# Eighty-four bursts of idle products between the expert layers of a four-layer sandwich kernel, in a new order of its pieces

## The reference, cut to what matters

```python
x = x + ln(L0_attn(ln(x)))   # Mamba scan, then a mixture of 8 experts, top 2
x = x + ln(L0_ffn(ln(x)))    # 64 small experts, top 8, and 2 shared ones
x = x + ln(L1_attn(ln(x)))   # WKV recurrence
x = x + ln(L1_ffn(ln(x)))    # ternary weight
x = x + ln(L2_attn(ln(x)))   # attention in a window of 32
x = x + ln(L2_ffn(ln(x)))    # one of 8 matrices by position
x = x + ln(L3_attn(ln(x)))   # Lorentz attention
x = x + ln(L3_ffn(ln(x)))    # 8 experts, top 2, and a shared one
```

```python
g, u = x2d @ gate_w[e].T, x2d @ up_w[e].T
out += wmat[:, e] * ((silu(g) * u) @ down_w[e].T)
```

## Time and profile before

| | |
|---|---|
| median of 3 runs | 1402.85 us (1395.88 to 1403.54) |
| the profiled execution | 1396.86 us |
| its span, first to last instruction | 1395.0 us |
| TensorE busy | 1118.2 us (80%) |
| VectorE busy | 964.1 us (69%) |
| ScalarE busy | 718.8 us (52%) |
| GpSimd busy | 599.6 us (43%) |
| mean granted TensorE clock | 0.915 |

### The profile page before, as it was taken

The page is one execution under the profiler, slowest core; times in us unless marked ns, Lnnn a source line. Parts: engine busy times, 40 slices in busy tenths (PEclk is TensorE's granted clock), DMA queues, the critical chain, the costliest instruction groups (busy, mean ns, idle before and its releaser), DMA issues.

```text
span 1395.0 us, 13322 instructions
## 1 busy us (share of the span) xinstructions
PE 1118.2 (80%) x3922; PEld 583.8 (42%) x3922; DVE 964.1 (69%) x2181; ACT 718.8 (52%) x1377; POOL 599.6 (43%) x420
## 2 busy tenths in 40 slices
PE   4766968796978797787877776878987899999796
PEld 1222323332333243333334534445463556656565
DVE  4965887678866885576777795747636535559787
ACT  6626663756347642534334425435561468746564
POOL 1941966178715873032014763543423121225222
PEclk8897979897998899698989999989998999999898
DMA  6000000000000001100010000000000100000000
GB/s 216 1 0 0 1 0 1 1 0 1 0 1 0 1 1 68 36 0 1 1 68 1 1 0 0 1 1 1 1 1 17 52 0 1 8 1 8 0 9 8
DMA packets 11271, 17.76 MB, mean 13 GB/s; under 512 B 1304, under 2 KB 7584, under 8 KB 10688
## 3 DMA queue, kind: packets, MB, share of 16 engines
q1 hardware_dynamic: 11200, 16.93, 3.7%
HBM read 15.88 MB, written 1.05 MB: 12 GB/s over the span
## 4 chain that ended last, share of the span: by engine, by line
PE 38%; DVE 11%; ACT 7%; issue 3%; POOL 3%; POOLq 0%; DVEq 0%; ACTq 0%
PE bankE L1878 6%; PE bankE L1263 4%; ACT b_pr L1161 2%; PE bankS L1841 2%; PE bankE L1795 2%; PE bankS L1795 2%; PE bankE L1325 2%; PE bankS L1826 2%; PE bankE L1284 1%; PE bankS L1798 1%; PE bankE L1798 1%; PE bankE L660 1%; PE bankS L1768 1%; PE bankE L615 1%; PE bankE L653 1%
## 5 line engine op out<-in xcount | busy, mean ns | idle before, releaser
L775 DVE TENSOR_TENSOR_SCAN hs<-dA,carry,bankS 128x512 f32<-128x512 f32 x118 | 144.4, 1265 | 3.0 <-DVE bankS L766 0.4
L351 POOL TENSOR_TENSOR hc<-hs,cb 128x1024 f32<-128x1024 f32 x51 | 120.2, 2356 | 33.3 <-DVE hs L775 31.8
L1753 ACT ACTIVATE c_h<-bankE,C 128x512 f32<-128x512 f32 x144 | 98.7, 687 | 52.7 <-PE bankE L1878 50.4
L1647 POOL TENSOR_TENSOR c_acc<-c_acc,c_tw 128x512 f32<-128x512 f32 x32 | 45.9, 1436 | 159.5 <-DVE c_tw L1972 159.4
L326 POOL TENSOR_TENSOR cv<-cv,hc 128x1024 f32<-128x1024 f32 x45 | 106.2, 2361 | 3.5
L467 ACT ACTIVATE sg<-bankE,C 128x512 f32<-128x512 f32 x80 | 54.9, 687 | 83.5 <-PE bankE L615 83.4
L1878 PE MATMUL bankE<-c_fH,c_w1H 128*128 128x512 f32 x144 | 81.1, 563 | 1.1 <-ACT c_h L1753 1.1
L660 PE MATMUL bankE<-hh,f 128*128 128x512 f32 x128 | 70.4, 631 | 10.0 <-DVE hh L882 10.0
L766 DVE TENSOR_TENSOR bankS<-dx,bankS 128x1024 f32<-128x1024 f32 x59 | 72.2, 1223 | 6.2 <-PE bankS L539 5.7
L420 ACT ACTIVATE dA<-dl,Aneg 128x512 f32<-128x512 f32 x118 | 74.3, 708 | 0.1
L578 PE MATMUL bankE<-h2T,wg 128*128 128x512 f32 x128 | 71.1, 638 | 3.6 <-ACT sg L448 1.4
(11 more groups left out here) (534 smaller groups left out, 2955.4 us busy)
## 6 DMA issues: line engine op xcount, KB each, us to landing
c_w<-in_w SPq DMA_DIRECT2D x1, 2304.0 KB, 8.9
X<-in_x SPq DMA_DIRECT2D x4, 256.0 KB, 4.0
wg<-in_gate_T SPq DMA_DIRECT2D x1, 1024.0 KB, 7.8
wu<-in_up_T SPq DMA_DIRECT2D x1, 1024.0 KB, 9.8
f<-in_w SPq DMA_DIRECT2D x1, 1024.0 KB, 7.5
out<-X SPq DMA_DIRECT2D x4, 256.0 KB, 2.3
b_wq<-in_Wqkv SPq DMA_DIRECT2D x1, 768.0 KB, 4.4
g<-in_sw SPq DMA_DIRECT2D x2, 256.0 KB, 3.5
```

The source lines that it names most:

```text
L351: pool.tensor_tensor(dst[:, :, :], hs[:, k % HS, :, :], cb[:, k % 2, :].unsqueeze(1).to_broadcast([P, HV, G]), ALU.mult).then_inc(s["hc_re ...
L775: V.tensor_tensor_scan(hs[:, k % HS, h, :], decay(i, k, q), drive[:, h, :], carry[:, k, h:h + 1], ALU.mult, ALU.add).then_inc(s["scan_done ...
L1753: act.activation(h[:, n % 3, :], E[k % 2][:, :], ACT.Gelu_apprx_tanh, bias=col("b1_3", k)).then_inc(s["fs_ready"], 1)
```

## The change

A new kind of piece, Z, belongs to TensorE alone: three products of a constant by a constant, written to `S[3]`, that nothing reads and that signal nothing. There are 24 of them (Z0 to Z23) for each of the groups 0, 1 and 2 and 12 (Z0 to Z11) for group 3, 84 in all. Z0 to Z11 stand behind L1 of their group, Z12 to Z23 behind L2. All other pieces are the same as before, in an order that was searched anew with the bursts in it, in all three lanes.

```diff
 ORDER = [(p[0], p[1:].split(".")[0], int(p.split(".")[1])) for p in """
...
-    aM9.0 ao4.1 aN5.1 aM10.0 an5.1 aM11.0 ao5.1 aN6.1 aM12.0 an6.1 aM13.0 ao6.1 aN7.1 an7.1 aM14.0 ao7.1 aM15.0 aA4.1 aA5.1 aA6.1 aL1.0
-    aL3.0 aA7.1 aN8.1 aL4.0 an8.1 ao8.1 aL5.0 aN9.1 an9.1 aR2.0 ao9.1 aU0.0 aN10.1 an10.1 aU1.0 aU2.0 ao10.1 aU3.0 aR5.0 aN11.1 an11.1
...
+    aM10.0 ao4.1 aN5.1 an5.1 aM11.0 aM12.0 aA3.1 ao5.1 aN6.1 aM13.0 aM14.0 an6.1 ao6.1 aM15.0 aL1.0 aA4.1 aA5.1 aL3.0 aN7.1 an7.1 aL4.0
+    aZ0.0 aZ1.0 ao7.1 aZ2.0 aZ3.0 aA6.1 aN8.1 aZ4.0 aZ5.0 aZ6.0 aZ7.0 an8.1 ao8.1 aL5.0 aN9.1 an9.1 aA7.1 aZ8.0 aZ9.0 ao9.1 aR2.0 aU0.0
...
@@ -255,6 +259,7 @@
     FOLD = 1
+    BURST = 3
     SPREAD = {2: (1, 0), **{2 * x_ - 1: (x_,) for x_ in range(2, E0N)}}
@@ -624,6 +629,9 @@
             elif p == "L2":
                 down1(e, N_U - 1)
                 pe.matmul(E[2][:, :], fb2[:, :], cwT[:, :], start=False, stop=True).then_inc(s["fo_ready"], 1)
+            elif p[0] == "Z":
+                for _ in range(BURST):
+                    pe.matmul(S[3][:, :], sel[:, 0, :], sel[:, 0:4, :].rearrange("p a b -> p (a b)"), start=True, stop=True)
             elif p == "L6":
```

More of the change, by code:

```diff
@@ L105 @@
[L105 to L120, removed]
@@ new lines @@
+    aU6.0 ao13.1 aN14.1 an14.1 aU7.0 ao14.1 aN15.1 aU8.0 aU9.0 an15.1 ao15.1 aU10.0 aU11.0 aU12.0 aB1.1 aU13.0 aB3.1 aB4.1 aU14.0 aB2.1
+    aF1.2 aU15.0 aU16.0 aF5.2 aU17.0 aU18.0 aF6.2 aU19.0 aF2.2 aF0.2 aL2.0 aF7.2 aF3.2 aF8.2 aR1.1 aZ12.0 aL6.0 aZ13.0 aZ14.0 aZ15.0 aZ16.0
+    aR3.1 aA0.2 aA1.2 aL7.0 aA2.2 aA3.2 aZ17.0 aZ18.0 aF9.2 aN0.2 an0.2 aM0.1 aZ19.0 ao0.2 aZ20.0 aZ21.0 aZ22.0 aR4.1 aZ23.0 aM1.1 aN1.2
+    an1.2 aM2.1 aM3.1 ao1.2 aN2.2 an2.2 aM4.1 aM5.1 ao2.2 aN3.2 an3.2 aM6.1 aM7.1 ao3.2 aN4.2 an4.2 aM8.1 aM9.1 ao4.2 aN5.2 an5.2 aM10.1
@@ new lines @@
+    aZ9.2 an8.3 ao8.3 aL5.2 aN9.3 an9.3 ao9.3 aR2.2 aU0.2 aU1.2 aU2.2 aR5.2 aN10.3 aZ10.2 an10.3 ao10.3 aN11.3 an11.3 aR6.2 aZ11.2 aU3.2
+    ao11.3 aN12.3 aU4.2 an12.3 aU5.2 ao12.3 aN13.3 aU6.2 an13.3 aU7.2 ao13.3 aU8.2 aN14.3 aU9.2 aU10.2 an14.3 aU11.2 ao14.3 aN15.3 aU12.2
+    an15.3 aU13.2 aU14.2 aU15.2 aU16.2 ao15.3 aB1.3 aU17.2 aB3.3 aB4.3 aU18.2 aU19.2 aB2.3 aL2.2 bP0.0 aR1.3 aL6.2 aZ12.2 aZ13.2 aZ14.2
+    aZ15.2 aZ16.2 bP1.0 aZ17.2 aZ18.2 aZ19.2 aL7.2 bP2.0 aR3.3 bP3.0 aR4.3 bP4.0 aM0.3 bP5.0 bK1.0 bK11.0 aZ20.2 aZ21.2 aZ22.2 bK2.0 bK3.0
@@ new lines @@
+    bH3.2 bA10.3 bW3.2 cG1.0 bO3.2 bQ0.3 bA1.2 bA11.2 bA12.2 cH0.0 cZ0.0 cZ1.0 bA3.2 bQ1.3 cE0.0 cZ2.0 cE1.0 cT0.0 bX0.2 bQ2.3 ct0.0 cZ3.0
+    cE2.0 cE3.0 cT1.0 bX1.2 bX2.2 bX3.2 bQ3.3 ct1.0 cT2.0 bX4.2 ct2.0 bX5.2 bX6.2 bX7.2 cT3.0 bA4.2 bA2.2 bC0.3 cS6.0 bc0.3 ct3.0 cZ4.0
+    cY0.0 bA13.2 bN0.3 bC1.3 bV0.3 cS7.0 bH0.3 bc1.3 bN1.3 cy0.0 cW0.0 bW0.3 cZ5.0 cE4.0 bO0.3 bC2.3 bV1.3 bH1.3 bc2.3 bW1.3 bO1.3 bN2.3
+    bC3.3 bV2.3 bH2.3 bc3.3 cV0.0 bW2.3 bN3.3 cZ6.0 cT4.0 bO2.3 bV3.3 bH3.3 bW3.3 ct4.0 bO3.3 bA1.3 bA11.3 cZ7.0 cE5.0 bA12.3 cX0.0 cT5.0
@@ new lines @@
+    cR3.2 cU2.2 cU3.2 cO1.1 cU4.2 cs8.0 cU5.2 cU6.2 cO2.1 cU7.2 cU8.2 cU9.2 cU10.2 cU11.2 cU12.2 cU13.2 cU14.2 cU15.2 cU16.2 cR0.3 cU17.2
+    cU18.2 cU19.2 cU20.2 cR1.3 cU21.2 cU22.2 cU23.2 cU24.2 cU25.2 cU26.2 cU27.2 cR2.3 cU28.2 cU29.2 cU30.2 cU31.2 cU32.2 cU33.2 cU34.2
+    cU35.2 cU0.3 cU1.3 cO0.2 cR3.3 cU2.3 cU3.3 cO1.2 cU4.3 cU5.3 cU6.3 cO2.2 cU7.3 cU8.3 cU9.3 cU10.3 cU11.3 cU12.3 cU13.3 cU14.3 cU15.3
+    cU16.3 cU17.3 cU18.3 cU19.3 cU20.3 cU21.3 cU22.3 cU23.3 cU24.3 cU25.3 cU26.3 cU27.3 cU28.3 cU29.3 cU30.3 cU31.3 cU32.3 cU33.3 cU34.3
@@ L149, in mamba_and_experts @@
+    cU35.3 cO0.3 cO1.3 cO2.3
+""".split()]
 def mamba_and_experts(s, X, C, col, S, E, ident, sel, half, dram, first_lane, second_lane, bank):
```

66 lines of the change are left out of this document (34 added, 32 removed).

## The result

The changed kernel takes 1420.62 us (median of 4 runs, 1418.04 to 1422.69), the kernel before 1403.19 us on the same chip. The ratio is 1.0137, with a 95% interval from 1.0108 to 1.0165: 19 us slower, outside the range and with the other sign.

What follows compares the result with a forecast made beforehand. Waits between TensorE and VectorE, with TensorE partly at half clock, were taken as the bound. Clock -20, bursts +5.5 and order -3.3 sum to -17.8 us, from 1402.85 to 1385 us; range 1362 to 1408 us.

Steps and rivals of the forecast that it cites:

- What bounds the kernel: Whole kernel: waits between TensorE (80% busy) and VectorE (69%), with TensorE at half clock for part of the span.
- The clock: Seven turns from one expert layer to the next: less TensorE work at half clock saves 20 us.
- the bursts: Same seven turns: bursts mostly fill TensorE's idle time; 0.5 us exposed in each of four, 1.2 in three, +5.5 us.
- Rival 2: Seven turns: the clock stays up but little of it is on the path; 1400 us, no change, chance 0.16.
- Rival 1: Seven turns: the clock falls despite the bursts, which run at half; 8.1 us lost per turn, 1417 us, chance 0.13.
- The order: Second turns: router work moved earlier saves 3.3 us; rest of the new order taken as 0, 10 us either side.
- Rival 3: Causal and last layers: the new order loses 15 to 25 us, giving 1400 to 1408 us, chance 0.08.
- What would show it: Seven turns mostly at full clock: mean about 0.95, router product about 1 us, first U 1.02, TensorE busy near 1143.
- three signs against: Bursts spaced 0.43 us; L5 or M1's gate product over 1 us later; longer time from the b pieces on.

## Why the prediction was wrong, point by point

**What bounds the kernel** held: waits between TensorE and VectorE, and a low clock behind the long ones.

**The clock** (-20 us) and **the bursts** (+5.5 us) sum to -14.5 us. In the new order they measured together -7.5 to -9 us, at 78 us less of half clock; so half of the expected sum came. In the old order the same bursts in the nearest places measured +25 us, and 62 others, put into the waits, -4 us; so the +5.5 us were a price of these places in this order and of no other. The estimate spread the gain over all seven turns. The sections show it in three and lie within 0.3 us in four: L1 to L2 of group 0 takes as long with the bursts as without, since the first `hh` comes at nearly the same time. Rival 2 was right for three of the four sections behind L1; the fourth, of group 3, won 2.6 us. Rival 1 was right in two turns, where the bursts ran at half: in group 1 L5 came 1.3 us and the first U 2.6 us later than without them, in group 3 the first U 3.6 us later. Neither section grew by more than 0.3 us by it. How much of the net is the clock's and how much the bursts' no run separates, since no kernel has the one without the other.

**The order**, the step that failed: "For all the rest of the order the trace gives no price; I take 0, with 10 us to either side". The whole term was -3.3 us; it measured +26 us, beyond its bound. The 3.3 us did not come either. The wait for the router's weights did fall in the changed kernel (from 11.5 us in four to 5.3 us in three), but mostly since bursts stand in it: with the order alone it was 3.48 and 3.21 us in the two like turns, before 3.95 and 4.42 us, and the weights came 1.1 and 5.2 us later after L2. And these are waits of a few us on one engine, while the pieces that moved with them are whole scan steps (3.7 us of VectorE, 4.7 us of GpSimd) and a Mamba front. The trace of before did give prices for those. The earlier trace rows show VectorE 92% busy in the first turn, so a step moved into it must delay what stands behind it by about its own 3.7 to 4.7 us (with that step alone moved, L5 and `c` each came 4.5 us later after L1), and I wrote that "VectorE does the same work", which is true of the engine and false for the path. The bound of 10 us was taken from waits to be saved, not from work that was moved. One step, the U row of one group and one Mamba front, each moved alone, cost 0.83%, 0.50% and 0.35%; that these moves make up the 26 us is not shown, since undoing one in the new order won nothing.

**Rival 3** (the order loses elsewhere, 15 to 25 us) had nearly the size and the wrong place: behind the last L2 the time did not grow (677.6 to 676.6 us). Its chance of 0.08 was the mistake that cost the range; it should have stood for lane a too, where pieces moved past an engine that was 92% busy. (Its upper end is a slip: 1385 + 25 is 1410, not 1408.)

**What would show it**: the router product, the first U and the wait at R3 of group 0 went as said; the mean clock reached 0.924, not 0.95, TensorE's busy time 1177.5, not 1143 us, since the bursts took 73.3 and not 55 us, 63 of the 252 products starting at half clock. And two of the three signs against came: bursts at a spacing of 0.43 us, and L5 2.3 us and the gate product of M1 2.4 us later. The third, more time from the b pieces on, came with 1.1 us only (849.8 us from L2 of group 2 to the end, before 848.7 us). Without bursts the gate product of M1 comes 25.2 us after L2, so the order caused this lateness, not the block of twelve.
